# Gathers of a state-space scan moved from its pair loop into its preparation on GpSimd

## What is computed

```
x = x + 0.5 * ffn(layernorm(x))     # 64 experts, 8 chosen for each token
x = x + attn(layernorm(x))          # a state-space scan, 64 heads, state 128 x 8
x = x + 0.5 * ffn(layernorm(x))     # the same experts
```

```
h[t] = a[t]*h[t-1] + b[t]*B[t-1]*x[t-1] + g[t]*B[t]*x[t];   y[t] = C[t] . h[t]
```

## Time and profile before

| | us |
|---|---|
| median of 3 runs (lowest, highest) | 3351.05 (3346.88, 3356.59) |
| the profiled execution, time | 3350.67 |
| the profiled execution, span | 3348.9 |
| TensorE busy | 2812.7 (84%) |
| VectorE busy | 2403.5 (72%) |
| ScalarE busy | 1820.8 (54%) |
| GpSimd busy | 1587.4 (47%) |
| granted TensorE clock, mean | 0.913 |

### The profile page before, as it was taken

One profiled execution on the slowest core, in us unless ns is written; L12 is line 12 of the kernel. 1 busy time (PEld: TensorE's weight loads), 2 busy tenths in 40 slices (PEclk: granted clock), 3 DMA queues, 4 the chain that ended last, 5 costly groups with the idle time before them and its releaser, 6 DMA issues.

```text
span 3348.9 us, 84316 instructions
## 1 busy us (share of the span) xinstructions
PE 2812.7 (84%) x28752; PEld 2145.2 (64%) x28752; DVE 2403.5 (72%) x3926; ACT 1820.8 (54%) x3740; POOL 1587.4 (47%) x1420
## 2 busy tenths in 40 slices
PE   4359987888888899999985999998899999659980
PEld 3348874666666666666763677776577777448870
DVE  5333454999999569899955899995699999433454
ACT  1136645666666266666623777772677776136650
POOL 2750441555555335565610566663256666170356
PEclk7579998898999899999987999998999999779995
DMA  9967974665665256566502666662566664467883
GB/s 392 311 198 247 294 243 136 185 192 168 183 192 157 75 149 170 161 171 173 144 4 92 182 181 173 178 172 62 154 170 177 177 184 123 169 214 250 275 286 118
DMA packets 315371, 609.75 MB, mean 182 GB/s; under 512 B 59152, under 2 KB 163728, under 8 KB 314128
## 3 DMA queue, kind: packets, MB, share of 16 engines
q1 hardware_dynamic: 290576, 539.83, 53.1%
q0 software_dynamic: 24576, 67.14, 6.4%
HBM read 446.25 MB, written 159.51 MB: 181 GB/s over the span
## 4 chain that ended last, share of the span: by engine, by line
PE 48%; DVE 16%; issue 11%; DMA 10%; POOL 9%; ACT 4%; SPq 2%; DVEq 1%; POOLq 0%; ACTq 0%
PE bank L64 16%; POOL xd L494 6%; PE bank L573 5%; PE bank L1200 4%; PE bank L1330 3%; DVE tmp L1278 3%; DMA ykq<-yd,ic 3%; PE bank L1396 3%; PE bank L1394 2%; PE bank L1370 2%; DVE xbc L1254 2%; DVE rot L1278 2%; DMA xh<-xd 2%; PE bank L564 2%; PE cs_sn L587 2%
## 5 line engine op out<-in xcount | busy, mean ns | idle before, releaser
L64 PE MATMUL bank<-xh,wb 128*128 128x512 f32 x2048 | 680.3, 413 | 64.6 <-ACT btr L1345 35.0
L64 PEld LDWEIGHTS bank<-xh,wb 128*128 128x128 f32 x2048 | 370.2, 191 | 181.1 <-ACT btr L1345 55.0
L1209 ACT ACTIVATE xbc<-bank,norm_w 128x512 f32<-128x512 f32 x512 | 350.8, 685 | 236.3 <-PE bank L64 229.4
L1286 POOL TENSOR_TENSOR rot<-rot,tmp 128x512 f32<-128x512 f32 x256 | 340.4, 1330 | 199.2 <-DVE tmp L1278 199.2
L64 PE MATMUL bank<-xl,wb 128*128 128x512 f32 x1024 | 407.0, 397 | 0.0
L649 DVE TENSOR_TENSOR hh<-sg,bank 128x96 f32<-128x96 f32 x384 | 97.7, 254 | 389.9 <-ACT sg L623 388.8
L1287 POOL TENSOR_TENSOR rot<-rot,tmp 128x512 f32<-128x512 f32 x256 | 360.3, 1408 | 0.0
L1298 POOL TENSOR_TENSOR sq<-cst,rho 128x512 f32<-128x512 f32 x128 | 133.5, 1043 | 462.1 <-DVE x L1014 326.7
L1303 POOL TENSOR_TENSOR xc<-xc,sq 128x512 f32<-128x512 f32 x128 | 163.2, 1275 | 384.4 <-DVE xwp L1265 384.4
L1278 DVE SCALAR_TENSOR_TENSOR rot<-xbc,bias,cs_sn 128x1024 f32<-128x1024 f32 x256 | 325.4, 1271 | 8.4 <-DVE xbc L1254 6.7
L1278 DVE SCALAR_TENSOR_TENSOR tmp<-xbc,bias,cs_sn 128x1024 f32<-128x1024 f32 x256 | 326.4, 1275 | 0.0
(11 more groups left out here) (291 smaller groups left out, 6107.3 us busy)
## 6 DMA issues: line engine op xcount, KB each, us to landing
wb<-watt_dram SPq DMA_DIRECT2D x96, 1024.0 KB, 7.7
rr_bc<-rr_dram SPq DMA_DIRECT2D x128, 512.0 KB, 5.8
yd<-ys SPq DMA_DIRECT2D x96, 512.0 KB, 3.9
wd<-w_down SPq DMA_DIRECT2D x384, 96.0 KB
watt_dram<-wb SPq DMA_DIRECT2D x32, 1024.0 KB, 5.4
dt_bc<-row_dram SPq DMA_DIRECT2D x256, 128.0 KB
al_bc<-row_dram SPq DMA_DIRECT2D x256, 128.0 KB, 3.7
xd<-xg SPq DMA_DIRECT2D x12, 2048.0 KB, 24.1
```

The lines of the kernel that those rows point to most:

```text
L64: ins = e.matmul(dst, a, m, start=start and c == 0, stop=stop and c == n - 1, skip_group_check=not (start and stop))
L1209: e.activation(xbc[j % 4][:, i, :], of(i)[:, :], ACT.Copy, scale=norm_w[:, i:i + 1])
L1286: e.tensor_tensor(R[:, 2 * ty, :], R[:, 2 * ty, :], tmp[:, 2 * ty + 1, :], ALU.subtract)
```

## The change

The gathers of scans 0 and 1 leave the pairs. `pairs_pool` calls the new `gather_prep_pool` in place of the memset of `acc4`. It uses four buffers `got`, gathers up to three rows ahead straight from `idx` (scans 0 and 1 have fixed numbers, so no column is copied), and does the weighting and the addition on GpSimd itself: row 0 of a tile is weighted into `acc4`, each other row is weighted in place and then added. VectorE's part is deleted. `stage`, used by the scatters of scans 2 and 3, becomes two of the `got` buffers, and the scatters' count of index copies starts at zero in scan 2. In both expert blocks `combined(i)` becomes max(128 + i, paced(i)) + 10.

```diff
-        acc4, ykq = keep[:, 4:8, :], sb("ykq", [P, D])
-        stage = [ykq, th_raw]
+        acc4 = keep[:, 4:8, :]
+        got = [sb(f"got{i}", [P, D]) for i in range(4)]
+        stage = got[0:2]
...
-        combined = lambda i: paced(i) + LATE
+        combined = lambda i: max(NRB + i, paced(i)) + LATE
...
-        a_gk = soft("a_gk")
+        a_gk = [soft(f"a_gk{i}") for i in range(4)]
...
-        def gather_turn_pool(e, b, n, q, j):
-            e.wait_ge(e_gc.sem, e_gc.at(n))
-            e.nop(nofuse=True)
-            index_pool(e, n, q, j, RT * TOPK + b * NP)
-            e.indirect_dma_start(ykq[:, :], None, yd, bass.IndirectOffsetOnAxis(ic[j % 2][:, 0:1], 0)).then_inc(a_gk.sem, 16)
...
-            e.scalar_tensor_tensor(acc, ykq[:, :], w, acc, ALU.mult, ALU.add).then_inc(e_gc.sem, 1)
+        def gather_prep_pool(e, b):
+            n, c, w = NP * b, RT * TOPK + NP * b, w8[:, :, :].rearrange("p t k -> p (t k)")
+
+            def row(i):
+                if n + i >= 4:
+                    e.wait_ge(e_gc.sem, e_gc.at(n + i - 3))
+                    e.nop(nofuse=True)
+                e.indirect_dma_start(got[i % 4][:, :], None, yd, bass.IndirectOffsetOnAxis(idx[:, c + i:c + i + 1], 0)).then_inc(a_gk[i % 4].sem, 16)
+
+            def add(i):
+                acc = acc4[:, i // TOPK, :]
+                e.wait_ge(a_gk[i % 4].sem, a_gk[i % 4].at((n + i) // 4 + 1))
+                e.nop(nofuse=True)
+                if i % TOPK == 0:
+                    e.tensor_scalar(acc, got[i % 4][:, :], w[:, c + i:c + i + 1], None, ALU.mult).then_inc(e_gc.sem, 1)
+                else:
+                    e.tensor_scalar(got[i % 4][:, :], got[i % 4][:, :], w[:, c + i:c + i + 1], None, ALU.mult).then_inc(e_gw.sem, 1)
+                    e.wait_ge(e_gw.sem, e_gw.at(n - n // TOPK + i - i // TOPK))
+                    e.wait_ge(e_gc.sem, e_gc.at(n + i))
+                    e.nop(nofuse=True)
+                    e.tensor_tensor(acc, acc, got[i % 4][:, :], ALU.add).then_inc(e_gc.sem, 1)
+
+            if b == 1:
+                e.wait_ge(e_tk.sem, e_tk.at(1))
+                e.nop(nofuse=True)
+            for i in range(3):
+                row(i)
+            for i in range(NP):
+                if i + 3 < NP:
+                    row(i + 3)
+                add(i)
...
-            index_pool(e, n, q, j, (b - SG) * NP)
+            index_pool(e, n - SG * NP, q, j, (b - SG) * NP)
...
-                if gathers(b):
-                    gather_turn_pool(e, b, n, q, j)
-                else:
+                if not gathers(b):
                     scatter_turn_pool(e, b, n, q, it, j)
...
-                if gathers(b):
-                    gather_turn_dve(e, b, n, q, it, j)
...
             if gathers(b):
-                e.memset(acc4, 0.0).then_inc(e_az.sem, 1)
+                gather_prep_pool(e, b)
             e.wait_ge(e_x12.sem, e_x12.at(b + 1))
```

More of the change, by code:

```diff
@@ L779, in ffn_sp @@
             blocks_sp(e, c)
-        e_gc, e_ic, e_az, e_tk, e_xst = (ev(n) for n in "e_gc e_ic e_az e_tk e_xst".split())
-        a_gk = soft("a_gk")
+        e_gc, e_gw, e_ic, e_tk, e_xst = (ev(n) for n in "e_gc e_gw e_ic e_tk e_xst".split())
+        a_gk = [soft(f"a_gk{i}") for i in range(4)]
         gathers = lambda b: isinstance(b, int)
```

## The result

The changed kernel takes 3361.28 us (median of 11 runs, 3354.42 to 3367.19) against 3351.05 (11 runs): a ratio of 1.0032, 95% interval 1.0022 to 1.0042, so slower by 0.3%. The forecast was slower by 0.7%. The profiled execution of the changed kernel took 3367.19 us with a span of 3365.4. It is the slowest of its 11 runs, so the two traces differ by 16.5 us where the medians differ by 10.2.

What follows compares the result with a forecast made beforehand. VectorE was taken to bound scan 0, TensorE scan 2, with scan 1 between. 3350.7 us plus 62 of late starts, minus 41.5 gained in the loops, plus 2 for a slower start gave 3374 us; 8 in 10: 3336 to 3404.

Steps and rivals of the forecast that it cites:

- 28 waits and issues: GpSimd in each preparation: wait on its own result, then issue a gather, 1.83 us each, 51.2 us in all.
- 28 waits of the addition for its weighting: GpSimd in each preparation: each addition waits 0.40 us for the weighted row, 11.2 us in all (4 to 21).
- 32 weightings: GpSimd in each preparation: multiplying 128x256 rows by their weights, 0.50 us each, 16.0 us in all (10 to 22.4).
- Sharing with VectorE: Preparation: GpSimd slowed where its operations meet VectorE's reads of SBUF, 6 us more (0 to 12).
- L = 109: GpSimd's time in us for gathering, weighting and adding 32 rows in each scan's preparation; 91 to 128 held possible.
- The lateness: Start of pair 0: scan 0 late by 21 us, scan 1 by 41.2, together 62, paid in full.
- Scan 1, 24.8 us: Loop of scan 1: without the weighted additions it reaches scan 2's pace, 24.8 us less (16.7 to 24.8).
- 31 x 0.54 = 16.7 us: Loop of scan 0: VectorE loses the weighted addition, 0.54 us a pair, 16.7 us less (12 to 20).
- The expert blocks, 0: Feed-forward part: weighted additions moved up to 18 blocks later cost nothing; 4 us if their cover failed.
- Rival 1: Preparations: GpSimd is ready sooner, 91 us of gathering a scan, net -13, 3337 us; chance 0.18.
- rival 2: Preparations: GpSimd is much slower, 125 us a scan, net +55, 3406 us; chance 0.12 together with the fourth rival.
- Rivals 3 and 4: Scans 0 and 1: lateness two thirds absorbed, 3333 us, chance 0.07; or loops gain nothing, 3413, 0.12 with rival 2.

## Why the prediction was right or wrong

The sign and the mechanism were right: GpSimd's preparation outlasts its idle time, both scans start late, both loops run faster. The size was not: +23 us forecast, +10.2 measured, 16.5 between the traces. The steps that failed are two terms of the sum, the weighting on GpSimd (0.50 us for 0.94) and the price of an addition in scan 0 (0.54 us a pair for 1.55). In order:

- **"Four issues back to back: ... 5.1 us"** and **"28 waits and issues: ... 51.2."** Right: 4.7, and 0.75 + 1.00 + 0.04 a row or 50.1, before the stretching (below).
- **"28 additions ... 0.70"**: 0.73.
- **"28 waits of the addition for its weighting ... 0.40"**: 0.17, 6 us too many.
- **"32 weightings ... I take the middle, 0.50: 16.0 us."** First failed term. It takes 0.94, 30 us in each scan, and is above the upper bound of 0.70, since I had bounded one input by two. An addition of 256 columns costs 0.73 and a product with a per-partition scalar costs more. The experiment without it moved the time by 57 us.
- **"Sharing with VectorE: ... 6 us more"**: instructions beside VectorE's were stretched, issues up to 2.03 us among them; over the undisturbed lengths it comes to 8 us in scan 0 and 4 in scan 1. **"I cost landings at nothing"**: the first row waited 1.61 and 1.94 us for its landing.
- **L = 109**: 120.5 and 116.3.
- **The lateness**, L - 89 in scan 0 and L - 68 in scan 1 by the prediction's sums: with the measured L that gives 31 and 48 us, and 30.5 and 49.2 were measured. The dependence chain behind the gathers was right, and that lateness is paid in full too. It had been forecast at 62 and is 79.7.
- **Scan 1, 24.8 us**: 21.2 in 28 pairs, which now take 405.4 us as scan 2's did (405.6), and 2.6 between its last pair and scan 2. Right.
- **"Scan 0: ... 31 x 0.54 = 16.7 us. ... not more than 20."** Second failed term, and the larger: 43.5 us in 28 pairs. I had read 0.54 as the price of the addition because it is the distance to the next start. The rows that I quoted for it held the rest of the price: the split behind it at 2.29 us against 1.22 alone. I put that down to GpSimd as such and not to the addition in front. Leaving the additions out, 67 us, and the halved rotations, 23 us, show that each further VectorE operation in that group costs about one GpSimd instruction of waiting.
- **The expert blocks, 0**: right.

So the lateness was forecast 17.7 us too small and the gain 23.2 too small: 22.5 + 17.7 - 23.2 - 0.5 for the rest = 16.5. That explains 6 of the 13 us by which the forecast missed the median. The other 6 are the distance of the profiled execution from the median of its runs; in its trace the time from the last pair of scan 3 to the end is 524.4 us, against 516 to 523 in the eleven other traces. That the forecast came as near as it did is luck: two errors, each about as large as the forecast itself, nearly cancelled. Rival 1 (GpSimd ready sooner) is refuted, rival 2's length of 125 was close, and its time of 3406 failed on the same gain as the forecast. Rivals 3 and 4 are refuted by the two pieces of each scan's distances.

## What to carry to other kernels

Work moved into the idle time of an engine paid here only up to the length of that idle time, and what the work takes there has to be measured for each instruction: one input was dearer than two. The price of an operation on a saturated engine wasn't the distance to the next start; look at the duration of the operation behind it, and compare it with the same operation elsewhere in the trace. Splitting the work by what an engine does well (GpSimd issues the gathers in 42 us, VectorE adds in its gaps) turned a loss of 0.3% into a gain of 2.1%.

## What the runs showed of the hardware

- While GpSimd had rotations in line, VectorE's operations with two inputs in SBUF took turns with GpSimd's instructions, one for one. The first of a group took 0.2 us more than alone (the split 1.42 against 1.22), each further one 1.07 us more beside 128x512 rotations (2.29 against 1.22; 1.49 against 0.42) and 0.53 more beside 128x256 ones (1.75 and 0.94; the first of the group then 0.48 more, 1.70 against 1.22). A memset of 128x512 on VectorE took 0.485 us each of 64 times, so it waited for nothing; the split right behind it waited in 2 of 26 pairs. The Trainium skill says in "GPSIMD Engine Reference", Key points, that the two engines share SBUF interfaces where VectorE has two SBUF inputs; the trace agrees, with the waits above beside it.
- A product with a per-partition scalar on GpSimd took 0.94 us at 128x256, an addition of two tensors 0.73. The Trainium skill's "GPSIMD Engine Reference", Engine selection, has one-input work at roughly line rate; the 0.3 us that the prediction estimated from it is a third of what the trace shows, and the measurement decides.
- On GpSimd, a wait for its own previous instruction took 0.17 us before a compute instruction and 0.75 before an indirect DMA. In the run with overlapped rows the first was gone, with one other instruction between; before the DMA, which there waited for the fourth-last addition, 0.16 us were left.
